# Experts with a gated unit: the first layer as three one-pass products, the up part's limit on ScalarE

## The reference, cut to what matters

```python
logits = jnp.einsum('bsh,he->bse', hidden_states, Wr) + br
topk_vals, topk_idx = jax.lax.top_k(logits, TOP_K)
router_scores = jax.nn.softmax(topk_vals, axis=-1)
gu = jnp.einsum('bsh,ehf->bsef', hidden_states, Wgu) + bgu     # 192 -> 384
gu = jnp.minimum(gu, LIMIT)                                     # LIMIT = 7
gate = gu[..., :I]
up = jnp.maximum(gu[..., I:], -LIMIT)
glu = gate * jax.nn.sigmoid(gate * ALPHA)
activated = (up + 1.0) * glu
down = jnp.einsum('bsei,eih->bseh', activated, Wd) + bd         # 192 -> 192
```

## Time and profile before

| | |
|---|---|
| median of three runs | 6769.15 us |
| the profiled execution's own time | 6724.65 us |
| its span, first to last instruction | 6722.8 us |
| mean granted TensorE clock over the span | 0.757 |
| PE busy | 4869.4 us (72%) |
| DVE busy | 4616.6 us (69%) |
| ACT busy | 2706.9 us (40%) |
| POOL busy | 1390.5 us (21%) |
| expert tiles of the touched stage | about 4901 to 5283 us of the span |

### The profile page before, as it was taken

How to read it: one execution, slowest core, us unless ns; L and a number is a source line. 1 busy time by engine, 2 the same in 40 slices (tenths; PEclk the granted TensorE clock), 3 DMA queues, 4 the chain that set the end, 5 groups by cost and what they waited for, 6 DMA issues and landing times. The chain is left out here.

```text
span 6722.8 us, 139374 instructions
## 1 busy us (share of the span) xinstructions
PE 4869.4 (72%) x46024; PEld 3804.2 (57%) x46025; DVE 4616.6 (69%) x10128; ACT 2706.9 (40%) x9057; POOL 1390.5 (21%) x1125
## 2 busy tenths in 40 slices
PE   5777777967777777777777777765089498419995
PEld 2333334755666566656665666555068376419995
DVE  4777774238999999999999999994267734312224
ACT  3343342224554545454555455543322133233331
POOL 1323322110000000000000000000655200166663
PEclk7777778986767676777676767665589799559997
DMA  8000000002111111121111111121122600221114
GB/s 144 7 5 8 5 3 6 0 8 76 71 71 65 69 68 71 65 71 65 71 69 68 66 70 71 65 71 27 65 71 76 113 0 6 73 67 45 46 46 137
DMA packets 226734, 370.27 MB, mean 55 GB/s; under 512 B 104818, under 2 KB 187355, under 8 KB 201028
## 3 DMA queue, kind: packets, MB, share of 16 engines
q1 hardware_dynamic: 200036, 309.26, 15.6%
q0 software_dynamic: 26112, 53.64, 2.4%
HBM read 287.04 MB, written 75.78 MB: 54 GB/s over the span
## 5 line engine op out<-in xcount | busy, mean ns | idle before, releaser
L2680 PE MATMUL l2a_g<-l2a_feat,l2a_onehot 128*128 128x33 bf16 x27648 | 783.1, 184 | 414.0 <-ACT l2a_values L2283 211.2
L2680 PEld LDWEIGHTS l2a_g<-l2a_feat,l2a_onehot 128*128 128x128 bf16 x27648 | 768.1, 101 | 484.6 <-issue 238.3
L2546 DVE TENSOR_REDUCE l2a_dots<-l2a_prod 128x144 f32<-128x2304 f32 x192 | 489.6, 2550 | 4.5
L1912 PE MATMUL l_y<-l_hc,l_selT 128*96 128x512 f32 x384 | 296.3, 866 | 264.2 <-POOL l_hc L1750 263.6
L2629 PE MATMUL l2a_s<-l2a_qkT 32*128 32x128 f32 (+1 forms) x1536 | 484.5, 451 | 0.0
L2652 PE MATMUL l2a_m<-main_ident,l2a_pv 128*96 128x128 f32 x2304 | 339.4, 319 | 148.6 <-DVEq L2487 148.6
L2652 PEld LDWEIGHTS l2a_m<-main_ident,l2a_pv 128*96 128x96 f32 x2304 | 331.4, 201 | 169.4 <-issue 166.1
L1750 POOL TENSOR_TENSOR l_hc<-l_hs,l_bc 128x512 f32<-128x512 f32 x192 | 243.6, 1269 | 718.8 <-DVE l_hs L1817 718.8
L2554 DVE TENSOR_SCALAR l2a_onehot<-l2a_spread,l2a_pos 128x4096 bf16<-128x4096 bf16 x288 | 360.8, 1281 | 43.7 <-DVE l2a_hd L2448 20.1
L2629 PEld LDWEIGHTS l2a_s<-l2a_qkT 32*128 32x128 f32 x1536 | 309.2, 249 | 86.0 <-issue 38.3
L713 PE MATMUL l3f_expert_h<-l3f_tT,l3f_w_own 96*128 96x256 f32 x2592 | 334.2, 288 | 8.6 <-POOL l3f_w_own L670 6.7
(11 more groups left out here) (408 smaller groups left out, 11353.8 us busy)
## 6 DMA issues: line engine op xcount, KB each, us to landing
l2a_spread<-l2a_idx_rows SPq DMA_DIRECT2D x192, 1024.0 KB, 4.7
rows_in<-main_zeros SPq DMA_DIRECT2D x1, 13824.0 KB, 82.7
l2f_xg<-rows_in SPq DMA_DIRECT2D x72, 192.0 KB, 2.5
l3f_xg<-rows_in SPq DMA_DIRECT2D x72, 192.0 KB, 2.5
l2f_combine_y<-rows_out SPq DMA_DIRECT2D x32, 384.0 KB, 3.8
l3f_combine_y<-rows_out SPq DMA_DIRECT2D x32, 384.0 KB, 4.8
l3f_w<-in_l3f_w SPq DMA_DIRECT2D x2, 4608.0 KB, 32.2
l_xT<-in_l_xT SPq DMA_DIRECT2D x16, 384.0 KB, 3.8
```

The source lines that it names most:

```text
L1912: nc.tensor.matmul(y_ps[:, :], selT[:, g, :], hc[:, g % 2, :], start=g == 0, stop=g == G - 1).then_inc(hc_used, 1)
L2546: nc.vector.tensor_reduce(dots[:, quad_of(s[2]), 0:NPROD], prod[:, :, :, :], AX.X, ALU.add).then_inc(S["dots_ready"], 1)
L2680: ins = nc.tensor.matmul(o[:, a * FEAT:a * FEAT + 2 * HS + 1], onehot[:, kt, at:at + P], feat3[:, s[1], kt, part, h, 0:2 * HS + 1], start= ...
```

## The change

`tT` and `wgu_own` become `F32R` and get one more dimension, for the high part (0) and the low part (1). F now has three products for each block and half: high weights by high rows, high weights by low rows, low weights by high rows. That is 24 weight loads and 24 matmuls, of one pass each.

- The high part of the weights is copied by ScalarE (new `own_weights` there, 96x768), the low part is subtracted by GpSimd (96x768, after `own_high`).
- The high part of the rows is ScalarE's copy as before, the low part is a new VectorE instruction (`low_rows`, 96x512).
- For the up part ScalarE computes relu(LIMIT - bias - x) from PSUM (`up_to_limit`, two instructions); VectorE's two L995 go, and its L1000 limits from the other side. The sign is made good in the last product.
- The orders change: ScalarE own(j+1), turned(j+1), up_to_limit(j), silu(j); GpSimd own(j+1), store(j-1), own(j+2), store(j); VectorE low_rows(j+1), clip(j), finish(j-1), low_rows(j+2), clip(j+1), finish(j). TensorE's order stays.

The diff, cut to its core:

```diff
-                                ins = nc.tensor.matmul(ps[u][:, c, :],
-                                                       wgu_own[:, u, h, (c0 + c) * HC:(c0 + c + 1) * HC],
-                                                       tT[:, u, h, :], start=h == 0, stop=h == 1)
+                                for wp, tp_ in ((0, 0), (0, 1), (1, 0)):
+                                    ins = nc.tensor.matmul(ps[u][:, c, :],
+                                                           wgu_own[:, u, wp, h, (c0 + c) * HC:(c0 + c + 1) * HC],
+                                                           tT[:, u, tp_, h, :], start=h == 0 and wp == tp_,
+                                                           stop=h == 1 and wp == 1)
...
+                def own_weights(r, u):                                   # ScalarE
+                    e = owner_of(act, plan, r * 2 + u)
+                    if not first_round(r):
+
+                        act.wait_ge(up_ready, r * 2 + u - 1)
+                        hold(act, act_held)
+                    nc.scalar.copy(wgu_own[:, u, 0, :, :],
+                                   wgu[:, :, bass.ds(e, 1), :].rearrange("p h a f -> p h (a f)")
+                                   ).then_inc(own_high, 1)
+
+                def up_to_limit(r, u):
...
+                    act.wait_ge(up_ready, j + 1)
+                    hold(act, act_held)
+                    for c in range(2):
+                        ins = nc.scalar.activation(up_rest[:, u, c, :], up_ps[u][:, c, :], ACT.Relu,
+                                                   bias=to_limit[:, bass.ds(e, 1), c:c + 1]
+                                                   .rearrange("p a c -> p (a c)"), scale=-1.0)
+                    ins.then_inc(up_half, 1)
...
                 with act.Fori(1, LAST + 1) as r:
+                    own_weights(r, 0)
                     turned(r, 0)
+                    up_to_limit(r - 1, 1)
                     silu_of(r - 1, 1)
+                    own_weights(r, 1)
                     turned(r, 1)
+                    up_to_limit(r, 0)
                     silu_of(r, 0)
...
-                    nc.gpsimd.tensor_copy(wgu_own[:, u, :, :],
-                                          wgu[:, :, bass.ds(e, 1), :].rearrange("p h a f -> p h (a f)")
-                                          ).then_inc(own_ready, 1)
+                    pool.wait_ge(own_high, r * 2 + u + 1)
+                    hold(pool, pool_held)
+                    nc.gpsimd.tensor_tensor(wgu_own[:, u, 1, :, :],
+                                            wgu[:, :, bass.ds(e, 1), :].rearrange("p h a f -> p h (a f)"),
+                                            wgu_own[:, u, 0, :, :].bitcast(F32), ALU.subtract).then_inc(own_ready, 1)
...
-                own_weights(1, 1)
                 store(0, 0)
                 with pool.Fori(1, LAST) as r:
+                    own_weights(r, 1)
+                    store(r - 1, 1)
                     own_weights(r + 1, 0)
-                    store(r - 1, 1)
-                    own_weights(r + 1, 1)
                     store(r, 0)
+                own_weights(LAST, 1)
...
+                def low_rows(r, u):                                      # VectorE
+                    dve.wait_ge(tT_high, r * 2 + u + 1)
+                    if not first_round(r):
+                        dve.wait_ge(up_ready, r * 2 + u - 1)
+                        hold(dve, dve_held)
+                    nc.vector.tensor_tensor(tT[:, u, 1, :, :].rearrange("p h t -> p (h t)"), tp[u][0:HC, :],
+                                            tT[:, u, 0, :, :].rearrange("p h t -> p (h t)").bitcast(F32),
+                                            ALU.subtract).then_inc(tT_ready, 1)
...
-                    for c in range(2):
-                        ins = nc.vector.tensor_scalar(up_in[:, u, c, :], up_ps[u][:, c, :],
-                                                      bgu[:, bass.ds(e, 1), 2 + c:3 + c].rearrange("p a c -> p (a c)"),
-                                                      LIMIT, ALU.add, ALU.min)
-                    ins.then_inc(up_half, 1)
                     dve.wait_ge(up_half, j + 1)
-                    nc.vector.tensor_scalar(up_in[:, u, :, :], up_in[:, u, :, :], -LIMIT, 1.0,
-                                            ALU.max, ALU.add).then_inc(up_clipped, 1)
+                    hold(dve, dve_held)
+                    nc.vector.tensor_scalar(up_in[:, u, :, :], up_rest[:, u, :, :], -1.0 - LIMIT, LIMIT - 1.0,
+                                            ALU.add, ALU.min).then_inc(up_clipped, 1)
...
+                low_rows(0, 0)
+                low_rows(0, 1)
                 clip(0, 0)
+                low_rows(1, 0)
                 clip(0, 1)
                 finish(0, 0)
-                with dve.Fori(1, LAST + 1) as r:
+                with dve.Fori(1, LAST) as r:
+                    low_rows(r, 1)
                     clip(r, 0)
                     finish(r - 1, 1)
+                    low_rows(r + 1, 0)
                     clip(r, 1)
                     finish(r, 0)
```

More of the change, by code:

```diff
@@ L835, in moe_glu_phase @@
         xg = m.sb("xg", [P, 2, 2, C])
-        tT = m.sb("tT", [HC, 2, 2, ETOK])
-        wgu_own = m.sb("wgu_own", [HC, 2, 2, 4 * HC])
+        tT = m.sb("tT", [HC, 2, 2, 2, ETOK], F32R)
+        wgu_own = m.sb("wgu_own", [HC, 2, 2, 2, 4 * HC], F32R)
+        to_limit = m.sb("to_limit", [HC, E, 2])
         gate_in = m.sb("gate_in", [HC, 2, 2, ETOK])
         up_in = m.sb("up_in", [HC, 2, 2, ETOK])
+        up_rest = m.sb("up_rest", [HC, 2, 2, ETOK])
         silu = m.sb("silu", [HC, 2, 2, ETOK])
@@ L854, in moe_glu_phase @@
         tp_ready = m.sem("tp_ready")
+        tT_high = m.sem("tT_high")
         tT_ready = m.sem("tT_ready")
+        limit_ready = m.sem("limit_ready")
+        own_high = m.sem("own_high")
         own_ready = m.sem("own_ready")
@@ L866, in moe_glu_phase @@
         pool_held = m.sem("pool_held")
+        act_held = m.sem("act_held")
+        dve_held = m.sem("dve_held")
         LAST = ETILES // 2 - 1
@@ L922, in turned @@
                     act.wait_ge(tp_ready, j + 1)
-                    nc.scalar.copy(tT[:, u, :, :].rearrange("p h t -> p (h t)"), tp[u][0:HC, :]).then_inc(tT_ready, 1)
+                    nc.scalar.copy(tT[:, u, 0, :, :].rearrange("p h t -> p (h t)"), tp[u][0:HC, :]
+                                   ).then_inc(tT_high, 1)
+                def own_weights(r, u):
[7 more added lines that the diff above has]
+                def up_to_limit(r, u):
+                    j = r * 2 + u
+                    e = owner_of(act, plan, j)
+                    if not first_round(r):
+                        act.wait_ge(up_clipped, j - 1)
+                    act.wait_ge(up_ready, j + 1)
[5 more added lines that the diff above has]
+                    ins.then_inc(up_half, 1)
                 def silu_of(r, u):
@@ L978, in _ @@
                 dve.wait_ge(weights_in, 64)
+                nc.vector.tensor_scalar(to_limit[:, :, :], bgu[:, :, 2:4], -1.0, LIMIT, ALU.mult,
+                                        ALU.add).then_inc(limit_ready, 1)
+                def low_rows(r, u):
+                    dve.wait_ge(tT_high, r * 2 + u + 1)
+                    if not first_round(r):
+                        dve.wait_ge(up_ready, r * 2 + u - 1)
[3 more added lines that the diff above has]
+                                            ALU.subtract).then_inc(tT_ready, 1)
                 def clip(r, u):
@@ L1008, in clip @@
                         dve.wait_ge(y_ready, j - 1)
-                    nc.vector.scalar_tensor_tensor(out=aT[:, u, :, :], in0=silu[:, u, :, :], scalar=1.0 / ALPHA,
+                    nc.vector.scalar_tensor_tensor(out=aT[:, u, :, :], in0=silu[:, u, :, :], scalar=-1.0 / ALPHA,
                                                    in1=up_in[:, u, :, :], op0=ALU.mult,
@@ L1022, in finish @@
                                             ALU.add).then_inc(ys_ready, 1)
+                low_rows(0, 0)
+                low_rows(0, 1)
                 clip(0, 0)
+                low_rows(1, 0)
                 clip(0, 1)
                 finish(0, 0)
-                with dve.Fori(1, LAST + 1) as r:
+                with dve.Fori(1, LAST) as r:
+                    low_rows(r, 1)
                     clip(r, 0)
                     finish(r - 1, 1)
+                    low_rows(r + 1, 0)
                     clip(r, 1)
                     finish(r, 0)
+                low_rows(LAST, 1)
+                clip(LAST, 0)
+                finish(LAST - 1, 1)
+                clip(LAST, 1)
+                finish(LAST, 0)
                 finish(LAST, 1)
```

8 lines of the change are left out of this document (6 added, 2 removed).

## The result

The changed kernel takes 6956.07 us (median of 4 runs, 6951.19 to 6963.47) against 6768.71 us for the kernel before: a ratio of 1.0277, interval 1.0259 to 1.0295. The prediction was 6957 us. The profiled execution took 6955.95 us.

The account below looks back on a forecast made before the run. It took TensorE to bound the touched stage at 5.19 us a tile; a 6.9 us ring with mixed clock makes 7.8, so (7.8 - 5.19) x 72 = +188 us on 6769 gives 6957 us, range 6865 to 7000.

Parts of the forecast that it names:

- The bound before and the saving: Touched stage: TensorE bounds it at 5.19 us a tile; F falls to 2.91 us, so TensorE needs 4.70.
- the second rival: Touched stage: TensorE stays the bound and gets faster, -35 us, 6734 us; chance 0.05.
- The moved work: VectorE, ScalarE, GpSimd: each engine's work, with a 0.85 us weights' copy and 1.82 us subtraction, fits in 4.70 us a tile.
- that rival: ScalarE: relu and silu displace each other's tables, two 1.28 us loads a tile, +65 us on top, 7022; chance 0.04.
- The ring: Touched stage: VectorE's and GpSimd's new orders make F(j+2) wait on a chain from F(j), 6.88 us a tile.
- the sum: The chain's links from F(j) to F(j+2) added up: 13.76 us for two tiles, 6.88 a tile.
- the port wait: VectorE against GpSimd's subtraction: L1051's place delayed, `aT` starts 0.1 to 0.2 us late, 6.95 us a tile.
- The clock: TensorE in the touched stage: waiting 2.2 us a tile drops the granted clock to 0.78, mean tile 7.8 us.
- the prediction's own formula: Touched stage: mean tile mixes 6.9 us at high clock with 9.4 at low, 1 / (0.56/6.9 + 0.44/9.4) = 7.8 us.
- Profiled execution and median: Whole kernel: the median lies 44.5 us above the profiled execution; +188 us applied to the median gives 6957.
- The signs: Changed profile: stage 500 to 600 us, clock 0.7 to 0.9, PE waiting for `wgu_own`, first DMA for `ys`.
- signs of being wrong: PE busy over 97%, waiting for `tT` or `aT`, clock 1.00 despite 2 us waits, or subtraction over 2.5 us.

Follow-up runs that it names:

- e11: e7 with SyncE loading the target rows one tile later (tile t-3 instead of t-2): 6729 us, ratio 0.9936 to the kernel before.
- e1: Changed kernel with GpSimd's old order, own(j+2), store(j-1), own(j+3), store(j): 6780 us, ratio 1.0022 to the kernel before.
- e4: Changed kernel with eight unneeded small TensorE products ahead of each F: 6891 us, ratio 1.0191 to the kernel before.
- e8: Changed kernel with TensorE's order T(j+1), F(j), S(j-1): 6893 us, ratio 1.0175 to the kernel before.
- e5: Kernel before the change, with the changed kernel's order on GpSimd alone: 6823 us, ratio 1.0068 to the kernel before.
- e9: Changed kernel with GpSimd subtracting 384 of 768 columns, the up part's low weights left at zero: 6939 us, ratio 1.0229 to the kernel before.
- e10: Changed kernel without L1051, the up part's lower limit and the + 1: 6972 us, ratio 1.0284 to the kernel before.
- e7: Changed kernel with GpSimd's old order and TensorE's order T(j+1), F(j), S(j-1): 6784 us, ratio 1.0006 to the kernel before.

## Why the prediction was right, step by step

**The bound before and the saving.** F took 2.77 to 2.80 us at the high clock (first load of the gate to first load of T), for the 2.91 forecast, and e11, where TensorE bounds the stage, shows 4.57 us a tile for the 4.70. The reading that TensorE alone bounded the kernel before holds. The -35 us of the second rival are there to be had (e11 has 43), but only after orders that the change doesn't have.

**The moved work.** ScalarE's copy of the weights measured 0.833 us (0.85 forecast), the subtraction 1.81 (1.82), both in all 72 tiles. One table load, as forecast; that rival is out.

**The ring.** Means over the tiles 10 to 63 of the changed kernel, from start to start, beside the terms of the sum:

| link | forecast | mean | least |
|---|---|---|---|
| F to T | 2.91 | 3.78 | 2.77 |
| T to ScalarE's copy | 0.85 | 0.90 | 0.75 |
| copy to `low_rows` | 0.62 | 0.80 | |
| `low_rows` to gate | 1.05 | 1.03 | |
| gate to `aT` | 1.60 | 2.30 | |
| `aT` to `ys` | 1.17 | 1.04 | |
| `ys` to first DMA | 1.44 | 1.47 | |
| DMA to subtraction | 2.25 | 2.32 | |
| subtraction | 1.82 | 1.81 | |
| its end to F | 0.05 | 0.40 | 0.07 |
| two tiles | 13.76 | 15.84 | |

e1 shows by itself that the ring is the cause: one exchange in one queue, and 2.55 of 2.77% are gone. The row-bound links (subtraction, DMAs, `ys`, the read of the expert's number) all came within 0.13 us.

**The mis-sized term: the port wait.** It was taken as 0.1 to 0.2 us for two tiles, by reckoning where L1051 would stand in a ring at the high clock. Gate to `aT` is 0.70 longer on the mean (median 1.64, at most 3.22). The wait goes with the clock, tile by tile. In the tiles 4 to 68 F is at the high clock in all even ones (F to T 2.77 to 2.80 us) and at least partly at the low clock in all odd ones (4.29 to 5.03). L1051 takes 1.5 to 2.3 us in 32 of the 33 even tiles and 0.41 us in every odd one. Behind a slow F it starts at least 2.41 us after the subtraction's start, so after its end; behind a fast F it meets it. The reckoning took every tile as equal; they alternate. In e4, where nearly every F is fast, gate to `aT` is 1.90 us, still 0.30 over the forecast. Copy to `low_rows` was short by 0.18. Some other links were shorter than forecast, so that the ring at the high clock, 7.03 us in e4, is only 0.15 us a tile over the sum's 6.88, 11 us in all.

**The clock.** Forecast 0.78 and 0.9 us a tile; measured 0.83 and 0.89 (e4). That the price agrees is in part luck, for the mechanism behind it was another. The prediction mixed whole tiles, 6.9 us at the high clock and 9.4 at the low one, where TensorE's own work would bound. But in the steady part the low clock never held for a whole tile, and no distance is near 9.4: all but one (10.47) are between 7.26 and 8.31 us. Beside e4 the links show what the low clock added, for two tiles: 0.97 us from F to T, 0.14 from T to the copy, 0.30 in the last link, but also 0.40 from gate to `aT`, the port wait's part. The last link grew because of a second chain that the prediction did not have: behind an F at the low clock, F to T 5.03, T to the copy 1.30, the copy to `low_rows` 0.80, `low_rows` 0.69 and 0.13 to the next F make 7.95 us for one tile, and in 21 of 65 tiles this comes after the subtraction. With the measured clock of 0.83 the prediction's own formula gives 1 / (0.66/6.9 + 0.34/9.4) = 7.6 us and a loss of some 173 us. The clock taken too low made up for what the formula and the ring left out, so 7.8 us was met by 7.92, and the 1 us between 6957 and the median is chance. Of the 188 us some 132 are the ring at the high clock (1.84 x 72) and some 64 the mixed clock (0.89 x 72); they add up to a little over the 186 measured in the stage, since its ends are not in the mean.

**Profiled execution and median.** The step that put the difference on the median held. The changed kernel's profiled execution lay at its median, that of the kernel before 44 us under its own. Spans of the two executions differ by 231 us; 186 are in the stage, the rest lies in untouched stages, 19 us before it and 26 after it. Who reads the two profiles alone would call the loss 231.

**The signs.** Stage length, clock, subtraction behind the second DMA, first DMA behind `ys`, `low_rows` behind ScalarE's copy, and the table load came as said. "PE waits for `wgu_own`" is true by the times, but the list names it in 13 tiles only. Of the signs of being wrong one came true in part: in 21 of 65 tiles F waits last for `tT`, that is for `low_rows`, all of them tiles that follow an F at the low clock.

**Who waits for whom.** The 1.74 and 2.80 us above end 0.30 and 0.56 us after the subtraction. The Trainium skill, SBUF — State Buffer, section Who interferes with whom, has the instruction that issues second wait for all of the other. The two ends agree that the wait is for the whole. By recorded starts, though, `aT` in e8 was first by 0.43 us and still waited; the trace doesn't show when either was issued. The starts in a timeline do not tell who gets the ports. In no run was it GpSimd that waited: its subtraction of 768 columns took 1.79 to 1.87 us in every tile of every run that has it. And the rule as the prediction quotes it, for two SBUF inputs, doesn't cover L1000 and L1051, which read one tensor in SBUF each; that they wait too is what their own rows show.

**What stays open.** By what the ports are given when both instructions come within half a microsecond, since VectorE waited each time. Why the clock falls in every second tile here. The part of e5's 46 us that is L1000's wait and not the ring's order alone was not separated; for that the copy would have to move off the shared ports.

## What to carry to other kernels

When an instruction's order in a queue changes, write down the ring that closes through all queues and divide its length by the tiles that it spans: each engine's sum was at most 4.7 us here, and the ring took 7. Keep the preparation for tile j+2 ahead of the store of tile j-1, since a store is the last link of a long chain. Price a wait of TensorE with its clock: idle 2 us in 8, the stage ran at 0.83, and the clock made a third of the damage. When a link is shortened and nothing comes of it, look for a second chain of nearly the same length (e9, e10). After a gain look at what feeds the faster engine (e7), since one load order hid it all.

## What was not expected of the hardware

- More work made the kernel faster: 1.9 us of needless products a tile took 58 us off (e4), the clock going from 0.83 to 0.98.
- The clock can alternate in step with the work: in the changed kernel F took 2.8 us in every even tile and 4.3 to 5.0 in every odd one, and VectorE's port wait fell on the even ones alone.
- A port wait is not bound to an instruction: with one of two left out (e10) the other waited, up to 2.05 us, and halving the other side (e9) moved what was left of it from L1051 to `aT`.
- A wait can be longer than the subtraction's 1.81 us: `aT` took up to 2.81 us in e8, 2.1 more than undisturbed.
